# x tiles loaded by eight transfers of 16 partitions; second tile behind Wk, initial memory and Wo behind Wv

## The reference

```
x = x + layernorm(attention(layernorm(x), Wq, Wk, Wv, Wo, betas, memory0, z0))
x = x + layernorm(ffn(layernorm(x), cn_w1.., gc_w1.., adaptive_range))

attention, for each of the 4 segments of 128 rows of a sequence:
  q, k, v = rows @ Wq, rows @ Wk, rows @ Wv            # (256 x 1024) each
  att_dot = softmax(mask(q k^T / 8)) v                 # within the segment
  att_mem = (elu(q)+1) M / ((elu(q)+1) Z)              # M starts at memory0, Z at z0
  M, Z   += (elu(k)+1)^T v, sum of (elu(k)+1)
  out     = (sigmoid(betas) att_mem + (1 - sigmoid(betas)) att_dot) @ Wo
```

## Time and profile before

| | us |
|---|---|
| median of 3 runs | 1091.38 (1090.75 to 1092.98) |
| the profiled execution, its own time | 1093.28 |
| its span, to which the rows below refer | 1091.5 |
| TensorE busy | 998.4 (91%) |
| VectorE, ScalarE, GpSimd busy | 778.1, 635.2, 577.5 |
| first matmul of a projection starts at | 20.89 |
| first matmul that reads Wo starts at | 61.54 |

### The profile page before, as it was taken

One profiled execution on the slowest core, in us unless ns is written; L12 is line 12 of the kernel. 1 busy time (PEld: TensorE's weight loads), 2 busy tenths in 40 slices (PEclk: granted clock), 3 DMA queues, 4 the chain that ended last, 5 costly groups with the idle time before them and its releaser, 6 DMA issues.

```text
span 1091.5 us, 20017 instructions
## 1 busy us (share of the span) xinstructions
PE 998.4 (91%) x7748; PEld 703.4 (64%) x7748; DVE 778.1 (71%) x1398; ACT 635.2 (58%) x1364; POOL 577.5 (53%) x687
## 2 busy tenths in 40 slices
PE   2999999999999999999999999999998888999971
PEld 1577777776777777777777777777676754433431
DVE  3869686868687877768696968696958444378675
ACT  4656565556565564647465646565655344577862
POOL 2456565446565663457474636474745332355573
PEclk9999999999999999999999999999999789899995
DMA  5200000000000000000000000000000002100015
GB/s 157 55 11 11 11 11 11 11 17 5 18 4 20 2 20 1 21 1 21 1 21 1 21 1 20 2 20 1 11 10 2 26 8 85 80 0 1 1 39 116
DMA packets 14989, 23.90 MB, mean 22 GB/s; under 512 B 5424, under 2 KB 7216, under 8 KB 14384
## 3 DMA queue, kind: packets, MB, share of 16 engines
q1 hardware_dynamic: 13644, 18.83, 6.0%
q10 hardware_dynamic: 1252, 3.80, 1.1%
HBM read 13.97 MB, written 8.65 MB: 21 GB/s over the span
## 4 chain that ended last, share of the span: by engine, by line
PE 69%; DVE 19%; POOL 4%; ACT 3%; issue 2%; DMA 1%; ACTq 0%; POOLq 0%; DVEq 0%
PE ps L1229 18%; PE ps L1335 11%; PE ps L1293 6%; PE ps L1270 5%; DVE arena L909 4%; PE ps L1299 3%; PE ps L1468 3%; PE ps L1481 3%; PE ps L1280 3%; PE ps L1320 3%; PE ps L1245 3%; PE ps L1463 2%; DVE arena L869 2%; PE ps L1307 2%; DVE arena L934 2%
## 5 line engine op out<-in xcount | busy, mean ns | idle before, releaser
L1229 PE MATMUL ps<-arena 128*128 128x512 f16 x1152 | 267.0, 382 | 7.4 <-DVE arena L886 5.3
L656 ACT ACTIVATE arena<-ps,arena 128x128 f32<-128x128 f32 x512 | 139.4, 387 | 98.1 <-DVE arena L934 98.1
L1229 PEld LDWEIGHTS ps<-arena 128*128 128x128 f16 x1152 | 110.4, 98 | 128.6 <-DVE arena L886 5.7
L909 DVE STREAM_TRANSPOSE arena<-ps 128x1024 f32<-128x1024 f32 x96 | 145.7, 1517 | 24.9 <-PE ps L1229 22.8
L464 POOL TENSOR_TENSOR arena<-arena 128x256 f32<-128x256 f32 x128 | 93.1, 728 | 126.2 <-DVE arena L944 84.9
L1293 PE MATMUL ps<-arena 128*128 128x65 f32 x1024 | 137.2, 278 | 5.9 <-ACT arena L663 4.8
L1293 PEld LDWEIGHTS ps<-arena 128*128 128x128 f32 x1024 | 128.6, 194 | 18.9 <-ACT arena L663 8.3
L861 DVE BATCH_NORM_STATS2 arena<-arena 128x6 f32<-128x256 f32 x100 | 36.9, 410 | 125.8 <-ACT arena L676 120.2
L1335 PE MATMUL ps<-arena 128*128 128x256 f32 x544 | 121.9, 382 | 0.0
L449 POOL TENSOR_TENSOR arena<-arena 128x512 f32<-128x512 f32 x48 | 73.2, 1525 | 86.8 <-ACT arena L649 86.8
L1335 PEld LDWEIGHTS ps<-arena 128*128 128x128 f32 x544 | 102.0, 190 | 15.7 <-ACT arena L670 0.8
(11 more groups left out here) (120 smaller groups left out, 1796.0 us busy)
## 6 DMA issues: line engine op xcount, KB each, us to landing
x_rows<-arena SPq DMA_DIRECT2D x17, 256.0 KB, 2.0
arena<-x_rows SPq DMA_DIRECT2D x4, 1024.0 KB, 7.9
arena<-in_L_attn_x_dram SPq DMA_DIRECT2D x62, 64.0 KB
out_dram<-arena SPq DMA_DIRECT2D x28, 128.0 KB, 2.9
arena<-in_L_attn_Wq_dram ACTq DMA_DIRECT2D x2, 512.0 KB, 12.1
arena<-in_L_attn_Wk_dram ACTq DMA_DIRECT2D x2, 512.0 KB, 15.0
arena<-in_L_attn_Wv_dram ACTq DMA_DIRECT2D x2, 512.0 KB, 17.9
arena<-in_L_attn_Wo_dram SPq DMA_DIRECT2D x8, 128.0 KB, 5.2
```

The lines of the kernel that those rows point to most:

```text
L656: last = act.activation(Pr[:, par, j, :], s_bank[:, par, j * P:(j + 1) * P], ACT.Exp, bias=negm[:, par, j:j + 1])
L909: dve.transpose(dst[:, d0:d0 + 32], bank.rearrange("p w (d c) -> p d w c", c=C)).then_inc(x_free, 1)
L1229: last = pe.matmul(bank[:, w, :], xc[:, lx, k, w * P:(w + 1) * P], W16[lw][:, k, i, :], start=(n == 0), stop=(n == 5))
```

## The change

Three things are changed. A tile of x is loaded by eight transfers of 16 partitions (one for each q and y) instead of four of 32, everywhere: the source of one is now 16 rows of 512 numbers, where it was 2 x 16 rows. At the start, SP asks for betas right behind its part of the first tile, waits for the second half of Wk, asks for the second tile, waits for the second half of Wv, and asks for the initial memory, z0 and Wo. The counts that `n_stats` waits for are doubled. Lines behind the change move by 1 or 2.

```diff
@@ blocks
             for q in range(4):
-                src = rows[b] if isinstance(b, int) else rows[bass.ds(b, 1)].rearrange(
-                    "b s q y h n -> (b s) q y h n")
-                yield tile[32 * q:32 * q + 32], src[s, q]
+                for y in range(2):
+                    src = rows[b] if isinstance(b, int) else rows[bass.ds(b, 1)].rearrange(
+                        "b s q y h n -> (b s) q y h n")
+                    yield tile[32 * q + 16 * y:32 * q + 16 * y + 16], src[s, q, y]
@@ sync
-                for dst, src in list(blocks(xrow[0], x_rows, 0, 0))[0:2]:
+                for dst, src in list(blocks(xrow[0], x_rows, 0, 0))[0:4]:
                     sp.dma_start(dst, src).then_inc(x_in[0], 16)
+                sp.dma_start(gcol, betas.rearrange("a h b e -> (a h b e)").rearrange("(p n) -> p n", p=P)
+                              ).then_inc(beta_in, 16)
+                sp.wait_ge(w_in[1][KT - 1], 16)
                 for dst, src in blocks(xrow[1], x_rows, 0, 1):
                     sp.dma_start(dst, src).then_inc(x_in[1], 16)
-                sp.dma_start(gcol, betas.rearrange("a h b e -> (a h b e)").rearrange("(p n) -> p n", p=P)
-                              ).then_inc(beta_in, 16)
+                sp.wait_ge(w_in[2][KT - 1], 16)
                 for par in range(2):
                     sp.dma_start(M0[64 * par:64 * par + 64, :, 0:DK],
...
-                sp.wait_ge(w_in[1][KT - 1], 16)
                 for e in range(8):
@@ scalar
-                for dst, src in list(blocks(xrow[0], x_rows, 0, 0))[2:4]:
+                for dst, src in list(blocks(xrow[0], x_rows, 0, 0))[4:8]:
                     act.dma_start(dst, src).then_inc(x_in[0], 16)
@@ vector
-                        n_stats((s + 2) % 4, bp * 64 + 64 * (1 + (s + 2) // 4), m + 3)
+                        n_stats((s + 2) % 4, 128 * (bp + 1 + (s + 2) // 4), m + 3)
-                n_stats(0, 64, 1)
+                n_stats(0, 128, 1)
-                n_stats(1, 64, 2)
+                n_stats(1, 128, 2)
```

## The result

The changed kernel took 1085.88 us (median of 6 runs, 1083.34 to 1087.43), the kernel before 1092.95 (6 runs). The ratio is 0.9933, with a 95% interval from 0.9914 to 0.9952: 0.67% faster. Measured once more, it took 1083.34 (1082.94 to 1084.52), ratio 0.9918 (0.9898 to 0.9937). The two intervals share 0.9914 to 0.9937, a gain of 6.9 to 9.4 us of 1092.95.

The account below looks back on a forecast made before the run. Bound at the start by Wq's second half, landing 13.21 us after asking because x crowds two DMA engines. First projection moves from 20.89 to 15.44: 1091.38 - 5.45 = 1085.9 us, range for 8 in 10 1083.9 to 1088.3.

Parts of the forecast that it names:

- The cause: Start: x's transfers use two of 16 DMA engines, which also carry weight shares, so Wq's second half takes 13.21 us.
- Rival A: Start: x stays on two engines, Wq lands at 13.1, gain only 3.3 us, total 1088.1; chance 6%.
- The check that explained the 16.36: Start, before the change: 256 KB per crowded engine at 19.6 GB/s take 13.1 us; from 2.8 this gives 15.9.
- Asking on ScalarE: Start: four requests ahead of Wq instead of two, 0.65 us each, move what follows by 1.3; table load ends at 8.95.
- the other end: Start: at about 0.4 us per request, table load ends at 6.9, second Wq conversion starts at 9.0, gain 7.4 us.
- Landing of Wq: Start: first half lands at 7.8, second at 9.5, at most 0.8 later; both before ScalarE wants them.
- Rival C: Start: splitting only costs; two more requests put Wq 1.3 us later, total 1092.7; chance 4%.
- The upper end that I gave the gain: Start: cheap requests of about 0.4 us give a gain of 7.4 us, total 1084.0.
- First tile: Start: x's first tile lands at 6.2, transposes end at 10.4, ScalarE takes them at 12.9; hidden with 2.5 us spare.
- Second tile, betas, memory, steps: Start and loop: tile there by 20.1, wanted 25.1; betas hidden; memory in time; eight step requests take 6.4, nothing gained.
- rival D: Start: second tile lands at 33.5, 8.4 us after VectorE wants it, total 1094.3; chance 3%.
- Rival B: Initial memory late: z0 takes 16.8 us again, ScalarE's copies start at 37.4 instead of 35.0, total 1088.3; chance 7%.

Follow-up runs that it names:

- Order alone: The kernel before with SP's new order of requests, tiles of x still in four transfers of 32 partitions; 1089.9 us, ratio 0.9971.
- spread alone: The changed kernel with SP's old order, tiles of x still in eight transfers; 1083.17 us, ratio 0.9915; measured again 1084.3, ratio 0.9926.

## Why the prediction was right

*The cause.* Two engines that carried x and a share of each weight half: shown. Order alone left x on two engines (0.13, 53 GB/s) and won 3.0 at the first projection; spread alone won 7.5. My working for x left on two engines with the new order gave 3.3 us. Rival A, that x stays on two engines, is out by the 121 GB/s and by the 16 increments for each transfer. The check that explained the 16.36 is weaker than it looks: it took 19.6 GB/s for each engine, and the 53 GB/s of the earlier trace rows are 26.5 for each of the two; with these it gives 12.5. It fits the order-only run well, though: the second half of Wq landed there at about 12.8 (9.4 us after 3.37), where the same working gave 13.1. That the two queues take turns, and how fast the crowded engines work meanwhile, no run shows.

*Asking on ScalarE.* This term was off in size. I took 0.65 us for a request and +1.3 for two more. Four of the new form took 1.83 us, and the two of the old form had taken 1.90 (1.25 and 0.62), so nothing was added; that 1.90 stood in the earlier trace rows. The six requests for weights behind them also got shorter, 3.02 us instead of 3.65. Together the table load ended at 6.94 where I had 8.95, 2.0 us off. The cheap price stood in the text as the other end and was the nearer one, but its 6.9 was luck: 0.4 for the four requests of x alone gives 7.3, and 0.4 for all ten 6.0.

*Landing of Wq.* Also off, and the other way: 5.34 and 4.3 us in two profiles, where 2.1 + 1.7 is 3.8. I had called it hidden; in the first profile ScalarE waited 1.03 for it. I had named such a wait as a sign of rivals A and C, and it came without either: the first half landed after 5.34 us, where it had taken 11.1 before. With both errors the first projection came at 14.35 and 13.40, for 15.44 forecast, and the gain there was 6.5 and 7.5 for 5.45. That the first six runs met the forecast median of 1085.9 was luck: the kernel before was itself 1.6 slower beside them (1092.95) than in the three runs that I started from (1091.38), and this covered a gain sized too small. Measured as a difference, the gain was 7.1 us (ratio 0.9933), or 9 in the later measurement, whose median of 1083.34 lies just under my range. The upper end that I gave the gain, 7.4, was just wide enough for the first and too short for the second. The mechanism held; the sizes of two terms did not.

*First tile.* It is there by 6.24, as reckoned, but I called it hidden with 2.5 us to spare, which held for ScalarE with its table loaded at 8.95. With the table at 6.97 in the second profile nothing is spare: VectorE's normalising of this tile ends at 9.12, the first half of Wq is converted by then, and the low parts of Wq start behind the normalising. GpSimd's memsets and this tile set the 13.40.

*Second tile, betas, memory, steps.* As reckoned. The second tile is there in time, and rival D has its price: late by 6.5 us, it eats the whole gain. Betas hid behind the 36 matmuls. Rival B is out: z0 lands in 2.8 to 3.2 us. Loads in the steps cost nothing; eight requests took 3.86 us (at 76.19) where I had 6.4.

*Rival C*, that splitting only costs, is out for 16 rows. Only the step from 16 to 8 rows costs, a microsecond at the first projection; against the kernel before even 8 rows win (0.9957).

*What stays open.* The 36 matmuls behind the start took from 9.37 to 10.78 us in the profiles of the kernels with spread tiles. In the first profile of the changed kernel the timeline up to 20.3 has

```profile
14.35 6.23 PE L1231 MATMUL ps<-arena 128*128 128x512 f16 x15 [3.99 <-DVE arena L888]
```

that is about 0.43 us for each 512 columns, the 1.2 GHz level, though the granted clock reads 1.00; later twelve take 2.59, 0.216 each, 2.4 GHz. So the rise comes after 14 matmuls there and, by the same two paces, after 8 where they took 9.44. The idle time ahead doesn't decide it: 3.05 us ahead of 9.44, 3.04 ahead of 10.77. That is 1.4 us of scatter that I did not explain. More lies near the end, where the granted clock differs for the same kernel. The changed kernel, first and second profile:

```profile
840.00:860.00 20.00, 17.22 (x116) 15.50 (x116) 6.53 (x17) 8.12 (x19) 5.43 (x9) 0.84 0.00 1
```

```profile
840.00:860.00 20.00, 16.83 (x123) 15.28 (x124) 7.92 (x18) 8.20 (x20) 6.75 (x11) 0.93 0.00 1
```

Between the stores at 757.87 and 912.94, and 755.40 and 909.13, lie 155.07 and 153.73 us. The later start (0.95), the matmuls (1.34) and this stretch (1.34) make 3.6 us; the spans differ by 3.2 (1084.9 and 1081.7).

Open too is what lies under the 13.40: letting VectorE start on the first tile ahead of GpSimd's memsets was tried only where the tile came late.

## What to carry to other kernels

Where a DMA share stands at a small fraction of 16 with a steady GB/s, count the engines: here a transfer whose outer dimension was 2 slowed everyone who had a share on the same two engines, and cutting it into pieces of 16 equal rows was worth more than the change of order. Reckon the price of a request by its form, plain or nested, and ask for what is needed first before the backlog of the large transfers, on whichever queue. When two edits relieve the same resource, test each alone; here the waits that came with the spread could have been left out.

## What the runs showed of the hardware that I had not expected

A transfer of 32 KB asked for while 3 MB stood on the other queue took 6.26 us to land; with 1 MB there (and 2 MB asked for behind it on its own queue) 5.13; and 1.8 to 2.2 where it was asked for ahead of the weights. In these runs a second queue did not keep a small urgent transfer clear of a large one.

At the start, a request for 16 rows of 512 numbers cost 0.46 us (four in 1.83), one for 2 x 16 rows 0.65 (four in 2.62; the first on ScalarE 1.25), one for 8 rows 0.35 (eight in 2.77).

The increments of the semaphore told the forms apart where the DMA share could not: 3, 16 and 9 for each transfer from a source of 2 x 16, 16 and 8 rows, which I read as 2, 16 and 8 engines.

Eight requests in the place of four also ended SP's 14.09 us stall in asking for the memory, even with the old order (longest 2.65 us for z0 in the spread-only kernel), and so did the new order with four (longest 1.82): the stall went with the two engines' backlog.
